# A vision tower with Sobel tokens: gx partly summed by accumulating transfers, and the group loops written out

## The reference, cut to what matters

```python
def _L0_tok_ref(x):
    Ix = _dwconv(x, kx)
    Iy = _dwconv(x, ky)
    G = jnp.hypot(Ix, Iy)
    return jnp.sum(G, axis=1)
h = h + attn(_layernorm(h))
h = h + ffn(_layernorm(h))
```

## Time and profile before

| | |
|---|---|
| median of 3 runs | 1555.92 us (1555.5 to 1556.84) |
| profiled execution, its own time | 1557.53 us |
| its span, first to last instruction | 1555.7 us |
| mean granted TensorE clock | 0.715 |
| busy: PE, PEld, DVE | 819.8, 649.4, 1365.3 us |
| busy: ACT, POOL | 713.9, 110.2 us |
| DMA bytes | 57.12 MB, 29.11 MB of them in POOL's queue |

### The profile page before, as it was taken

The page is one execution under the profiler, slowest core; times in us unless marked ns, Lnnn a source line. Parts: engine busy times, 40 slices in busy tenths (PEclk is TensorE's granted clock), DMA queues, the critical chain, the costliest instruction groups (busy, mean ns, idle before and its releaser), DMA issues.

```text
span 1555.7 us, 12724 instructions
## 1 busy us (share of the span) xinstructions
PE 819.8 (53%) x3334; PEld 649.4 (42%) x3334; DVE 1365.3 (88%) x2078; ACT 713.9 (46%) x1288; POOL 110.2 (7%) x154
## 2 busy tenths in 40 slices
PE   3565000366639742456639643356639653486544
PEld 1233000355537632345528532245538542375433
DVE  7999997899999999899999999899999999522576
ACT  2221242354477633265467544155557553243562
POOL 0000000002102000002111000002011000000000
PEclk7887555767669866667569866577568876698866
DMA  8000500003304510104224510104133010100001
GB/s 200 4 10 14 115 0 0 1 12 63 65 10 72 106 41 1 29 1 75 45 30 66 111 41 1 29 1 75 25 50 61 14 41 1 28 1 0 0 0 27
DMA packets 33994, 57.12 MB, mean 37 GB/s; under 512 B 6602, under 2 KB 23930, under 8 KB 32250
## 3 DMA queue, kind: packets, MB, share of 16 engines
q0 software_dynamic: 21024, 29.11, 11.6%
q1 hardware_dynamic: 12314, 26.31, 7.4%
q10 hardware_dynamic: 576, 0.79, 0.2%
HBM read 22.84 MB, written 4.25 MB: 17 GB/s over the span
## 4 chain that ended last, share of the span: by engine, by line
DVE 28%; issue 24%; PE 18%; ACT 13%; DMA 1%; DVEq 0%; SPq 0%; ACTq 0%
DVE arena L541 8%; DVE arena L538 6%; PE psum L1666 5%; PE psum L1678 4%; DVE arena L910 2%; PE psum L1760 2%; PE psum L1810 1%; ACT arena L1325 1%; PE psum L1782 1%; DVE red L554 1%; ACT arena L1462 1%; ACT arena L1206 1%; ACT zT L1478 1%; ACT arena L1472 1%; DVE small L538 1%
## 5 line engine op out<-in xcount | busy, mean ns | idle before, releaser
L538 DVE TENSOR_TENSOR arena<-arena 128x768 f32<-128x768 f32 (+2 forms) x537 | 489.8, 967 | 16.6 <-ACT arena L1244 9.4
L541 DVE SCALAR_TENSOR_TENSOR arena<-arena 128x768 f32<-128x768 f32 (+2 forms) x224 | 201.4, 948 | 0.1
L1678 PE MATMUL psum<-zT,w1q 128*128 128x257 f32 x512 | 146.7, 425 | 18.5 <-DVE gpad L905 13.7
L1678 PEld LDWEIGHTS psum<-zT,w1q 128*128 128x128 f32 x512 | 109.1, 216 | 42.9 <-DVE gpad L905 18.1
L1666 PE MATMUL psum<-gpad,win 128*128 128x257 f32 x288 | 81.2, 423 | 37.4 <-ACT gpad L1337 37.4
L541 DVE SCALAR_TENSOR_TENSOR arena<-img 128x768 f32<-128x768 f32 x92 | 83.1, 949 | 15.8 <-DMA img<-x 8.7
L1277 ACT ACTIVATE arena<-arena 128x768 f32<-128x768 int16 x32 | 26.8, 843 | 150.4 <-DVE arena L541 150.1
L1782 PE MATMUL psum<-arena 128*128 128x257 f32 x128 | 48.1, 540 | 87.2 <-ACT arena L1440 66.0
L1666 PEld LDWEIGHTS psum<-gpad,win 128*128 128x128 f32 x288 | 60.3, 213 | 50.8 <-ACT gpad L1337 41.0
L514 POOL DMA_DIRECT2D h<-others x60 | 51.7, 862 | 393.9 <-DVE others L541 325.6
L1206 ACT ACTIVATE arena<-arena 128x256 f32<-128x256 f32 x65 | 23.3, 409 | 117.6 <-DVE arena L541 68.5
(11 more groups left out here) (226 smaller groups left out, 2051.6 us busy)
## 6 DMA issues: line engine op xcount, KB each, us to landing
img<-x SPq DMA_DIRECT2D x36, 258.0 KB, 6.9
h<-others POOLq DMA_DIRECT2D x60, 128.0 KB, 2.7
arena<-nrows_mem POOLq DMA_DIRECT2D x18, 384.0 KB, 4.4
arena<-arena POOLq DMA_DIRECT2D x18, 384.0 KB, 4.1
arena<-img POOLq DMA_DIRECT2D x18, 384.0 KB, 5.0
out<-out SPq DMA_DIRECT2D x16, 256.0 KB
img<-x SPq DMA_DIRECT2D x48, 64.5 KB, 6.3
win<-w_in SPq DMA_DIRECT2D x4, 768.0 KB, 5.0
```

What stands on the lines that cost most here:

```text
L538: return v.tensor_tensor(o, a, b, op)
L541: return v.scalar_tensor_tensor(out=o, in0=a, scalar=s, in1=b, op0=op0, op1=op1)
L1678: ins = mm((A0, A1, B0, B1)[i % 4][:, 0:S], w1q[:, k, t * P:(t + 1) * P], zT[:, k, b, :], start=(k == 0), stop=(k == DT - 1))
```

## The change

In pairs 1 to 3 of groups 1 to 3, gx is built negated. In the pair before, VectorE writes a back sum into tmp[f][1] at slot 4 (behind a wait for hisq, since tmp[f][1] was the quotient) and a front sum into a room of its own at slot 5: zT for the first two pairs, onehot and the last rows of h9 for the third. POOL adds an image row and then the front to tmp[f][1]; VectorE subtracts the last image row at the start of the pair, waiting for gx_sums. gy moves to tmp[f][5], its edge rows to slot 3. So ScalarE copies nrows ahead of slot 2 and the negated edges ahead of slot 3. To leave tmp[f][5] free the step of the ratio writes over r, and the square of x1 goes to tmp[f][6]: it now waits for root_rest, counted by the operation that last read tmp[f][6], and s1 moves behind slot 7, after the use of that square. This part of hypotenuse holds for group 0 too. All four group loops become Python loops; settle's column wraps at 46.

```diff
+        def front(i, f):
+            if i < PAIRS - 2:
+                room = zT.rearrange("p t b n -> p (t b n)")[:, f * CH * W:(f + 1) * CH * W]
+            elif f == 0:
+                room = onehot[:, :, :].rearrange("p r n -> p (r n)")[:, 0:CH * W]
+            else:
+                room = h9[:, ROWS - CH:ROWS, :].rearrange("p r w -> p (r w)")
+            return room.rearrange("p (c w) -> p c w", c=CH)
...
-            def carried_gy(g, i):
+            def carried_sums(g, i):
...
-                    pool.dma_start(tmp[f][1], nrows[:, f], accum_op=ALU.add).then_inc(gy_sums[f], 16)
+                    pool.dma_start(tmp[f][5], nrows[:, f], accum_op=ALU.add).then_inc(gy_sums[f], 16)
                 for f in range(2):
+                    pool.wait_ge(backs_out, count + f + 1)
+                    pool.dma_start(tmp[f][1], img[:, :, 2 * i + f + 2, 0:W], accum_op=ALU.add).then_inc(gx_sums[f], 16)
+                for f in range(2):
+                    pool.wait_ge(gy_sums[f], at_y + 16)
+                    pool.dma_start(tmp[f][5], edge[:, (2 * i + f) % 4], accum_op=ALU.add).then_inc(gy_sums[f], 16)
+                for f in range(2):
+                    pool.wait_ge(gx_sums[f], at_x + 16)
+                    pool.wait_ge(fronts_out, count + f + 1)
+                    pool.dma_start(tmp[f][1], front(i - 1, f), accum_op=ALU.add).then_inc(gx_sums[f], 16)
+                for f in range(2):
+                    pool.wait_ge(gy_sums[f], at_y + 32)
+                    pool.dma_start(tmp[f][5], img[:, :, 2 * i + f + 2, 2:2 + W], accum_op=ALU.add).then_inc(gy_sums[f], 16)
...
                 for f in F:
-                    rsq, b, mx, y0, x1, xsq, t = tmp[f]
+                    x1, t = tmp[f][4], tmp[f][6]
                     dve.wait_ge(rstep, n2 + f + 1)
                     u(stt(t, short(x1), 2.0 / STEP, sh16[:, f], ALU.mult, ALU.mult))
                 for f in F:
                     rsq, t = tmp[f][0], tmp[f][6]
-                    u(tt(rsq, rsq, t, ALU.subtract))
-                for f in F:
-                    x1, xsq, s1 = tmp[f][4:7]
-                    u(stt(s1, short(x1), 1.0 / STEP, sh16[:, f], ALU.mult, ALU.add))
+                    u.row(f)
+                    tt(rsq, rsq, t, ALU.subtract).then_inc(root_rest, 1)
                 slot(7)
                 for f in F:
-                    rsq, xsq = tmp[f][0], tmp[f][5]
+                    rsq, xsq = tmp[f][0], tmp[f][6]
                     dve.wait_ge(rstepsq, n2 + f + 1)
                     u(tt(rsq, rsq, xsq, ALU.subtract))
+                for f in F:
+                    x1, s1 = tmp[f][4], tmp[f][6]
+                    u(stt(s1, short(x1), 1.0 / STEP, sh16[:, f], ALU.mult, ALU.add))
...
                 def with_carry(k):
-                    if k == 5 and i < PAIRS - 1:
-                        for f in F:
-                            edge_row(tmp[f][1], 2 * i + f + 4).then_inc(carried, 1)
+                    nxt = 2 * i + 2
+                    if i < PAIRS - 1:
+                        if k == 3:
+                            for f in F:
+                                edge_row(tmp[f][5], nxt + f + 2).then_inc(carried, 1)
+                        if k == 4:
+                            for f in F:
+                                dve.wait_ge(hisq, n2 + f + 1)
+                                stt(tmp[f][1], px(nxt + f + 1, 0), 2.0, px(nxt + f, 2), ALU.mult, ALU.subtract).then_inc(backs_out, 1)
+                        if k == 5:
+                            for f in F:
+                                stt(front(i, f), px(nxt + f + 1, 2), -2.0, px(nxt + f, 0), ALU.mult, ALU.add).then_inc(fronts_out, 1)
+                    if k == 8 and i == PAIRS - 2:
+                        dve.wait_ge(gx_sums[1], ((g - 1) * (PAIRS - 1) + i) * GX_SUMS + 32)
                     slot(k)
...
+                else:
+                    slot(-2)
+                    for f in F:
+                        dve.wait_ge(gx_sums[f], ((g - 1) * (PAIRS - 1) + i - 1) * GX_SUMS + 32)
+                        tt(tmp[f][1], tmp[f][1], px(2 * i + f + 2, 2), ALU.subtract).then_inc(gx_ready, 1)
+                    slot(-1)
...
-            with dve.Fori(1, GROUPS) as g:
+            for g in range(1, GROUPS):
...
                 def with_carry(k):
-                    slot(k)
-                    if k == 3 and i < PAIRS - 1:
+                    if k == 2 and i < PAIRS - 1:
                         for f in F:
                             s.activation(nrows[:, f], img[:, :, 2 * i + f + 2, 2:2 + W], ACT.Copy, scale=-1.0).then_inc(neg_rows, 1)
-                    if k == 6 and i < PAIRS - 2:
+                    if k == 3 and i < PAIRS - 2:
                         for f in F:
                             act.wait_ge(carried, g * (2 * (PAIRS - 1)) - 2 * (PAIRS - 1 - i) + f + 1)
-                            s.activation(edge[:, (2 * i + f) % 4], tmp[f][1], ACT.Copy, scale=-1.0).then_inc(neg_edges, 1)
+                            s.activation(edge[:, (2 * i + f) % 4], tmp[f][5], ACT.Copy, scale=-1.0).then_inc(neg_edges, 1)
+                    slot(k)
...
                 for f in F:
-                    x1, xsq = tmp[f][4:6]
-                    act.wait_ge(rstep, n2 + f + 1)
+                    x1, xsq = tmp[f][4], tmp[f][6]
+                    act.wait_ge(root_rest, n2 + f + 1)
                     s.activation(xsq, short(x1), ACT.Square, scale=1.0 / STEP).then_inc(rstepsq, 1)
```

More of the change, by code:

```diff
@@ L127, in tower_kernel @@
 def tower_kernel(nc, x, cls_tok, w_in, b_qk, b_v, w_out, b_out, w1, conv_w, conv_b, w2, const, out):
-    U_STEPS = 56
-    CARRIED_STEPS = 50
+    U_STEPS = 54
+    CARRIED_STEPS = 40
     NORM_STEPS = 50
@@ L133, in tower_kernel @@
     IMG_IN = 16 * 2 * GB * CH
+    GX_SUMS = 32
+    NEG_ROWS = 6
     FIRST_IN = 16 * GB * CH
@@ L335, in tower_kernel @@
         gy_sums = [sem("gy_sums_0"), sem("gy_sums_1")]
+        gx_sums = [sem("gx_sums_0"), sem("gx_sums_1")]
+        backs_out = sem("backs_out"); fronts_out = sem("fronts_out"); root_rest = sem("root_rest")
         maxima = sem("maxima"); recips = sem("recips")
@@ L463, in _ @@
             group(0, first=True)
-            with sp.Fori(1, GROUPS - 1) as g:
+            for g in range(1, GROUPS - 1):
                 group(g)
@@ L474, in _ @@
             nc.gpsimd.memset(ones_row, 1.0).then_inc(ones_set, 1)
-            def carried_gy(g, i):
-                at = ((g - 1) * (PAIRS - 1) + i - 1) * 48
-                count = ((g - 1) * (PAIRS - 1) + i) * 2
+            def carried_sums(g, i):
+                pairs_done = (g - 1) * (PAIRS - 1) + i - 1
+                at_y, at_x, count = pairs_done * 48, pairs_done * GX_SUMS, pairs_done * 2
+                negs = (g - 1) * NEG_ROWS
                 for f in range(2):
-                    pool.wait_ge(neg_rows, count - 1 + f)
+                    pool.wait_ge(neg_rows, negs + 2 * i - 2 + f + 1)
                     if i < PAIRS - 1:
@@ L509, in _ @@
                     if g > 0 and row % 2 == 0 and row < ROWS - 2:
-                        carried_gy(g, row // 2 + 1)
+                        carried_sums(g, row // 2 + 1)
                     pool.wait_ge(hypots, g * ROWS + row + 1)
@@ L525, in settle @@
             def settle():
-                settled[0] += 1
+                settled[0] = settled[0] % 46 + 1
                 v.memset(idle[:, settled[0]:settled[0] + 1], 0.0)
@@ L711, in hypotenuse @@
                 for f in F:
-                    nl, q, mx, r, hsq, qr, t = tmp[f]
-                    u(tt(qr, short(q), r, ALU.add))
+                    q, r = tmp[f][1], tmp[f][3]
+                    u(tt(r, short(q), r, ALU.add))
                 for f in F:
-                    nl, q, mx, r, hsq, qr, t = tmp[f]
+                    nl, qr, t = tmp[f][0], tmp[f][3], tmp[f][6]
                     u(tt(t, nl, qr, ALU.mult))
@@ L798, in magnitude_rows @@
                         tt(gy, gy, px(f + 2, 2), ALU.subtract).then_inc(gy_ready, 1)
-                slot(-2)
-                for f in F:
-                    u(stt(tmp[f][0], px(2 * i + f + 1, 2), 2.0, px(2 * i + f, 0), ALU.mult, ALU.subtract))
-                for f in F:
-                    u(stt(tmp[f][2], px(2 * i + f + 1, 0), -2.0, px(2 * i + f, 2), ALU.mult, ALU.add))
-                slot(-1)
-                for f in F:
-                    u(tt(tmp[f][2], tmp[f][2], px(2 * i + f + 2, 0), ALU.subtract))
-                for f in F:
-                    u(tt(tmp[f][0], tmp[f][0], tmp[f][2], ALU.add))
-                for f in F:
-                    u.row(f)
-                    tt(tmp[f][0], tmp[f][0], px(2 * i + f + 2, 2), ALU.add).then_inc(gx_ready, 1)
-                hypotenuse(u, n2, i, with_carry, [t[0] for t in tmp], [t[1] for t in tmp])
+                if i == 0:
+                    slot(-2)
+                    for f in F:
+                        u(stt(tmp[f][0], px(f + 1, 2), 2.0, px(f, 0), ALU.mult, ALU.subtract))
+                    for f in F:
```

(21 more changed lines are left out.)

20 lines of the change are left out of this document (10 added, 10 removed).

## The result

| kernel | median, us | ratio to before (95% interval) | profiled span, us |
|---|---|---|---|
| before | 1556.84 | 1 | 1555.7 |
| changed | 1561.3 | 1.003 (1.0019 to 1.0041) | 1560.3 |

The forecast was 1549.4 us, with a range of 1538 to 1561. The time lies just above the range, where the rival C stood (1560.2 us). The ratio leaves out one execution of the kernel before, of 1582.24 us, which was in a slower state.

A forecast was written before the change was run, and what follows sets the result against it. VectorE bounds the kernel, busy 88%, except where ScalarE's silu behind TensorE's feed-forward work pins pair 3. Groups -1.0, group 0 +0.9, loops -6.4: -6.5 us, so 1551.0 profiled, median 1549.4 us; range 1538 to 1561.

The forecast's parts named there:

- rival C: TensorE's clock falls in the gap before tile 12: 3.6 us a group, 10.8 in all, 1560.2 us; chance 0.18.
- M to F: From selection's first MAX8 on VectorE to the start of pair 2's feed-forward matmuls: forecast 6.3 us shorter a pass.
- F to S: From the feed-forward matmuls' start to VectorE's start on pair 3's hypotenuse: forecast 4.6 us longer a pass.
- loops: VectorE's stands at the group loop's entry and two jumps back vanish when written out: -6.4 us in all.
- pair 3's wait: VectorE waits for ScalarE's root square, now ahead of s1, in pair 3: +1.35 us a group.
- S to M: From VectorE's start on pair 3's hypotenuse to the next selection's first MAX8: loops -6.4, pair 3's wait +4.05 us.
- tail: From the fourth selection's first MAX8 to the end of the span: forecast no change.
- The pin at S: VectorE's start on pair 3's hypotenuse comes 46.9 us behind the feed-forward matmuls' start whatever VectorE does, held by ScalarE's silu.
- The gaps of 1.85 and 2.75 us: TensorE idles ahead of tile 10 and tile 12, between the feed-forward matmuls' start and the second silu.
- The nrows copies: ScalarE copies ahead of the first feed-forward tiles: cost nothing; were those tiles at full clock, 1.3 us a group.
- I take 1.8 us of waiting: At pair 1's start, VectorE waits 1.8 us for TensorE's pick between own_heads and context; hypotenuse 1 moves -3.0 us.
- the late root: ScalarE's root square waits for root_rest: pair 3's hypotenuse 4.6 us later behind feed-forward start, plus 1.35 us in pair 3.

The follow-up runs named there:

- experiment 1: The kernel before with only its group loops written out as Python loops; 1551.18 us, ratio 0.9963 to before.
- experiment 3: The changed kernel with the root's square early, written into the negated images' rows, and s1 back ahead of slot 7; 1533.79 us, ratio 0.9851 to before.
- Experiment 2: The kernel before with written-out loops and the late root's square, no transfers added, gx computed as before; 1563.33 us, ratio 1.0042 to before.
- Experiment 7: The kernel of experiment 3 with the root's square late again in pair 2 alone; 1551.68 us, ratio 0.9969 to before.
- experiment 8: The kernel of experiment 3 with the root's square late again in pair 0 alone; 1538.1 us, ratio 0.9877 to before.
- experiment 9: The changed kernel with TensorE computing first-layer tile 13 twice and tile 15 three times, as filler in its gaps; 1557.42 us, ratio 1.0006 to before.

## Why the prediction was wrong

Its sum by stage was: M to F -6.3 us a pass (-18.9), F to S +4.6 (+13.8), loops -6.4 and pair 3's wait +4.05 in S to M (-2.35), group 0 +0.9, tail 0. That is -6.5 us. Measured, in the same order: -12.0, +16.4, -3.5, +0.2 ahead of the first M, +3.5. So the 11.1 us by which the sum was off are 6.9 in M to F, 2.6 in F to S and 3.5 in the tail, less 1.9 in the other two.

**Right.** The pin at S, and that VectorE's gain turns into waiting there (12 us forecast, 14.35 in the third pass). ScalarE's square at F+26.9 (F+26.8). The gaps of 1.85 and 2.75 us (1.76 and 2.50). S at F+51.5 (51.2 in the pass at full clock). The nrows copies ahead of tiles at full clock: the gap of 1.48 us at 1170.67 is this. It cost nothing at S, though, where the prediction would have had 1.3 us a group: S is at F+52.89 in the second pass, where these tiles ran at half clock in part, and at F+52.87 in the third, at full clock. ScalarE's square came later anyway. Group 0's +0.9 (its end moved from 271.19 to 271.94 us, 0.75). Pair 3's wait of 1.35 us (1.24). The loop heads: experiment 1's S to M is 3.4 and 3.6 us shorter in the passes that have one behind them. No wait for gx_sums, though the transfers land later than I took them, the page's median in us at the end:

```profile
arena<-img POOLq DMA_DIRECT2D x36, 384.0 KB, 7.4
...
arena<-arena POOLq DMA_DIRECT2D x18, 384.0 KB, 8.6
arena<-zT POOLq DMA_DIRECT2D x12, 384.0 KB, 8.4
```

7.4 to 8.6 us against the 5.0 of the earlier trace rows: within the doubled landing that was my upper bound.

**Wrong: "F: -6.3 us"**, 6.9 us of the 11.1 missing. It was -4.2, -4.25 and -3.6. The step that failed is "I take 1.8 us of waiting" for TensorE's pick: the three waits were 4.14, 3.10 and 6.64 us. TensorE idled 2.76 us ahead of the scores in each pass and worked at half clock behind it, in the third pass through scores, weighted values, keys and values (granted clock 0.50 from 1064 to 1076 us):

```profile
1063.35 3.80 PE L1828 MATMUL psum<-arena 128*128 128x257 f32 x8 [2.76 <-ACT arena L1486]
...
1073.42 3.79 PE L1781 MATMUL psum<-xT,win 128*128 128x257 f32 x8
1077.01 3.19 PE L1787 MATMUL psum<-win,xT 128*128 128x256 f32 x8
1080.03 0.53 PE L1864 MATMUL psum<-cst,arena 128*128 128x32 f32 x4
```

In the third pass of the kernel before the scores took 2.00 us and the values 1.89. Ahead of the gap ScalarE waited 3.49 us for the late square of pair 0, and behind the square, at once, came the copies of keys that TensorE needed:

```profile
1058.97 1.71 ACT L1339 ACTIVATE arena<-arena 128x768 f32<-128x768 int16 x2 [3.49 <-DVE arena L560]
1060.59 0.83 ACT L1463 ACTIVATE arena<-psum,bin_col 128x257 f32<-128x257 f32 x2
```

The late square makes that gap, but it does not make the wait. In experiment 3, with the square early in every pair, the gap ahead of the scores is 0.7 to 0.8 us, yet they start no earlier, 72.2 to 73.6 us behind M in both kernels, since TensorE stands 3.4 to 6.0 us for a copy of VectorE just ahead of that. They take 3.47 to 3.80 us, and VectorE still waits 3.88, 4.01 and 3.02 us for the pick. TensorE and VectorE in its second pass:

```profile
702.99 3.59 PE L1829 MATMUL psum<-arena 128*128 128x257 f32 x8 [0.79 <-ACT arena L1487]
...
717.52 0.23 DVE L1067 COPY arena<-psum 128x64 f32<-128x64 f32 x1 [4.01 <-PE psum L1865]
```

Experiment 2, with the late square but gx computed as before, has no wait for the pick in any pass: the wait shows once the six gx operations between own_heads and context are gone. The prediction saw that, and missed the size. It had keys_values start 2.7 us later, all of it from ScalarE's copies. Counted from M, keys_values starts 3.6, 4.7 and 5.7 us later than before, and 3.1, 3.2 and 4.5 with the square early; 1.5 to 1.8 of that are the scores alone, at half clock with the late square or without (here 0.50 from 703 to 706 us). VectorE takes the pick at M+87.0, 87.0 and 89.5 us in the changed kernel and at 86.6, 86.9 and 86.8 with the square early: the lateness is worth 0.5, 0.1 and 2.7 us there.

Behind the pick there is a second term of the clock. The prediction took 5.84 us for the output sums, as in all three passes of the kernel before. In every kernel with the transfers, F follows the pick by 86.5 to 86.6 us where they take 5.8 us, and by 84.9 where they take 4.15. The changed kernel had 5.84, 5.84 and 4.15. Experiment 7 has M to F 6.5, 6.0 and 6.1 us below before, which looks like the forecast, but its output sums took 4.15 us in all three passes; with the 5.84 of the forecast it would be 4.3 to 4.8 us (an estimate). So even without the late square there, the forecast of F was nearly 2 us a pass too good.

**Wrong: the clock behind the second gap**, 1.7 us in each of two passes; F to S as a whole was 2.6 us longer than forecast. Rival C named this place and set the point from which it decides between 3.33 and 3.59 us of idling. The trace has half clock behind 2.52 and 2.50 us, in the second and third pass, and full clock behind 2.50 in the first: no length of this gap alone decides. Its price was 1.7 us, not the 2.9 for a slow restart that C took. So C's total was right to 1.1 us by luck: its 10.8 us are terms that measured 3.4, and it had nothing for M to F or the tail.

**Wrong: the tail at nothing**, 3.5 us. Its code is untouched, and VectorE is busy there for the same 106.6 us in the first 220 us. TensorE has its same 616 matmuls there, but is busy 138.0 us with them where it was 131.4. Up to the last group's F the tail is 4.5 us longer, behind it 1.0 us shorter. The stretch from 20 to 40 us behind the fourth M, before and after (columns as above), has the clock at 1.00 and at 0.81, and 92 matmuls against 76:

```profile
1356.47:1376.47 20.00, 14.81 (x92) 12.87 (x91) 5.24 (x11) 11.29 (x28) 0.00 (x0) 1.00 0.00 1
```

```profile
1357.53:1377.53 20.00, 15.96 (x76) 13.33 (x74) 5.24 (x11) 10.36 (x24) 0.00 (x0) 0.81 0.00 1
```

Over the twelve kernels, whose tails have the same code, it took 218.8 to 224.2 us, and its length goes with the granted clock. Experiments 7 and 8 have the same clock in each of the first eleven stretches of 20 us and the same 218.93 us; experiments 3 and 9 have another row of clocks, the same in both, and the same 224.20 us. That it is TensorE's clock is read from the profiles; no run here forced the tail's clock, so why it falls in one kernel and not in another stays open.

**Right in kind, missed in size: the late root.** It stood in the sum at 4.6 + 1.35 us a pass, 18 us. Taking it away gave 27.5 us (experiment 3). In the profiled executions it is 22.5 us over the passes: 13.7 in F to S, of which 3.4 are the half clock behind the gap, 3.8 in S to M, and 5.0 in M to F, of which 4.3 are TensorE's clock (1.7 in the output sums of the second pass, 2.6 on the way to the pick in the third). The medians of experiments 7 and 8 add up to 22.2 us for pairs 2 and 0, and pair 3's waits of 1.24 us to 3.7 more. Without the late square the same transfers and loops are 1.5% faster than the kernel before: they did their part, and the reordering that freed a buffer for them took it away. In experiment 3 the square went into the rows of the negated images, free just then, so the late square was not needed.

## What to carry to other kernels

When VectorE gets faster, look first at the engine that feeds the next pin, here ScalarE's fixed order: a step that comes 3.5 us later on it costs whatever stands behind it, in each stage that it serves, not only where it is waited for. When operations leave an engine, price what they covered on the others, here TensorE's way to the pick, at both of its clocks. A buffer reused at the price of a later producer is a change in schedule; price it alone, and look for a buffer that is free by its dates. Where TensorE has gaps of 2 to 3 us, keep a price for half clock behind each in the range, and some us for the untouched rest of the kernel, for its clock shifts with the schedule ahead of it.

## What the runs showed of the hardware

- The same gap of 2.50 us in the same code was followed by full clock in one pass and by half clock in another (granted clock 1.00 throughout; 0.75, then 0.50). Experiment 7 repeats it: 2.52 us full, 2.51 and 2.54 us half. With the gap at 0.78 us, filled with repeated matmuls, the clock stayed full in all three, and the kernel was 3.9 us faster with more work in it.
- The same 18 matmuls of the output sums took 4.15 or 5.84 us, by pass and kernel, and moved all behind them by 1.7 us.
- An unchanged tail of some 220 us varied by 5.4 us between kernels. Differences of 0.2 to 0.3% between profiled executions of this kernel can't be read without the granted clock beside them.
- The stand of 3 us of VectorE at each loop's head left with the jumps (S to M 130.2 us to 126.8). The Trainium skill, Advanced Engine Details and Errata, section Control Flow Timing, gives about 51 ns for a jump and 108 ns for a compare-and-branch. The measured stand is some twenty times those two together (0.16 us); the trace does not agree with them as the whole cost of a loop's head, which is what the prediction said.
